# A second ScalarE activation for the high half of gelu in the last stage of a Macaron block

## The reference

```
bw1 = _binarize(w1)
h = jnp.einsum('bsd,hd->bsh', x, bw1) + b1
h = jax.nn.gelu(h, approximate=False)
bw2 = _binarize(w2)
out = jnp.einsum('bsh,dh->bsd', h, bw2) + b2
```

## Time and profile before

| what | value |
|---|---|
| median of 3 runs | 1490.82 us (1489.05 to 1491.58) |
| the profiled execution, its own time | 1486.6 us |
| its span, first to last instruction | 1484.8 us |
| PE busy | 1425.5 us (96%) |
| DVE busy | 1281.6 us (86%) |
| ACT busy | 1119.9 us (75%) |
| POOL busy | 942.8 us (64%) |
| mean granted clock of TensorE | 0.995 |

### The profile page before, as it was taken

One profiled execution on the slowest core, in us unless ns is written; L12 is line 12 of the kernel. 1 busy time (PEld: TensorE's weight loads), 2 busy tenths in 40 slices (PEclk: granted clock), 3 DMA queues, 4 the chain that ended last, 5 costly groups with the idle time before them and its releaser, 6 DMA issues. The chain is left out here.

```text
span 1484.8 us, 26133 instructions
## 1 busy us (share of the span) xinstructions
PE 1425.5 (96%) x7022; PEld 1010.8 (68%) x7022; DVE 1281.6 (86%) x2936; ACT 1119.9 (75%) x2618; POOL 942.8 (64%) x956
## 2 busy tenths in 40 slices
PE   6999999999889999999999999999999998999998
PEld 4555566555467777777777777777666666777776
DVE  7776676854689999999999999999999999788785
ACT  4554456548999999999999999999999965233333
POOL 0234322433189999999999999999999998300000
PEclk9999999999899999999999999999999999999999
DMA  8224437454766656666566656666545358464510
GB/s 278 85 83 149 148 129 194 142 164 145 240 191 187 183 162 180 185 175 179 154 175 186 183 163 173 175 171 182 127 112 120 99 134 245 139 208 150 185 56 29
DMA packets 232329, 236.33 MB, mean 159 GB/s; under 512 B 46296, under 2 KB 198040, under 8 KB 232184
## 3 DMA queue, kind: packets, MB, share of 16 engines
q1 hardware_dynamic: 231240, 233.34, 55.0%
q10 hardware_dynamic: 944, 1.31, 0.2%
HBM read 136.31 MB, written 98.56 MB: 158 GB/s over the span
## 5 line engine op out<-in xcount | busy, mean ns | idle before, releaser
L1377 DVE TENSOR_TENSOR_SCAN h<-decay,banks 128x308 f32<-128x308 f32 (+1 forms) x820 | 718.1, 882 | 0.9 <-issue 0.9
L1151 POOL TENSOR_TENSOR hc<-h,bc 128x640 f32<-128x640 f32 x410 | 592.7, 1446 | 0.0
L1200 PE MATMUL banks<-hc,w_ident 128*128 128x320 f32 (+1 forms) x1664 | 522.8, 437 | 0.1
L1269 ACT ACTIVATE tb<-dtc,a 128x320 f32<-128x320 f32 (+1 forms) x832 | 418.0, 558 | 0.0
L1200 PEld LDWEIGHTS banks<-hc,w_ident 128*128 128x128 f32 x1664 | 284.0, 191 | 66.6 <-POOL hc L1151 0.3
L1291 ACT ACTIVATE decay<-tb 128x640 f32<-128x640 f32 x410 | 296.1, 726 | 0.0
L1140 POOL TENSOR_TENSOR rc<-qs,w_mhalf 128x1 f32<-128x1 f32 x410 | 225.7, 551 | 80.2 <-DVE qs L1360 53.0
L1186 PE MATMUL banks<-ub 128*128 128x176 f32 x1640 | 272.6, 288 | 3.5 <-DMA ub<-scratch_ub 3.5
L1179 PEld LDWEIGHTS banks<-sc_ss,sc_ones 128*128 128x128 f32 x820 | 123.3, 189 | 143.2 <-ACT sc_sq L1280 141.1
L1186 PEld LDWEIGHTS banks<-ub 128*128 128x128 f32 x1640 | 216.8, 193 | 4.0 <-issue 2.5
L1367 DVE TENSOR_SCALAR banks<-h,rc 128x28 f32<-128x28 f32 (+1 forms) x820 | 176.1, 261 | 1.6 <-POOL rc L1140 1.4
(11 more groups left out here) (135 smaller groups left out, 1759.0 us busy)
## 6 DMA issues: line engine op xcount, KB each, us to landing
ub<-scratch_ub SPq DMA_DIRECT2D x410, 107.5 KB
bc<-scratch_blk SPq DMA_DIRECT2D x205, 160.0 KB, 3.5
scratch_ub<-turned SPq DMA_DIRECT2D x64, 512.0 KB, 3.6
scratch_ub<-spread SPq DMA_DIRECT2D x64, 176.0 KB, 2.4
scratch_xc<-xc SPq DMA_DIRECT2D x8, 1024.0 KB, 4.8
scratch_sg<-sg SPq DMA_DIRECT2D x8, 1024.0 KB, 5.9
piece<-scratch_u SPq DMA_DIRECT2D x32, 256.0 KB, 4.2
q_ys<-scratch_y SPq DMA_DIRECT2D x8, 1024.0 KB, 5.7
```

The costliest lines, as they stand in the source:

```text
L1151: pool.tensor_tensor(hc[:, pl % 2, :, at * S:(at + 1) * S] .rearrange("p (c b n) e -> p c b n e", c=KE, b=B)[:, :, b], state(m)[:, :, 0:S] ...
L1200: mm = pe.matmul(banks[:, y_bank(p), 0:KE * B * wide], w.ident[:], rhs, start=(n == 0), stop=(n == N - 1))
L1269: act.activation(tanh_rows(c, r), dtc[:, c % 2, k * B:(k + 1) * B, 0:blocks_of(c) * S].rearrange("p b (k e) -> p k b e", e=S), ACT.Tanh, s ...
L1377: dve.tensor_tensor_scan(state(m).rearrange("p r e -> p (r e)")[:, part], decay[:, m % DRING, part], psI[m % B][:, part], 0.0, ALU.mult, A ...
```

## The change

ScalarE gets a second kind of activation in the last stage: `high_g(i, m)`, which copies `gf` of block m as it is into the high half of g. In `gelus` it is issued for block m-1 after the gelu of block m, and for block 7 after the loop. The wait for `dn_done` goes with it. VectorE's `split_g` loses the cast and its waits and keeps the subtraction, which waits for `split_hi`, now raised by ScalarE. The orders of TensorE, GpSimd and SyncE are as they were, and so is the place of each `split_g` in VectorE's order.

```diff
@@ scalar @@
+        def high_g(i, m):
+            act.wait_ge(gelu_done, i * KH + m + 1)
+            if i >= 1 and m == 0:
+                act.wait_ge(dn_done, KD * i)
+            act.activation(g[:, 0, m, :], gf[:, m % GF, :], ACT.Copy).then_inc(split_hi, 1)
+
         def gelus(i):
             for m in range(KH):
                 act.wait_ge(up_done, i * KH + m + 1)
@@
                 act.activation(gf[:, m % GF, :], psM[:, m % 2, :], ACT.Gelu, bias=w.b1[:, m:m + 1],
                                scale=w.a1[:, m:m + 1]).then_inc(gelu_done, 1)
+                if m >= 1:
+                    high_g(i, m - 1)
+            high_g(i, KH - 1)
@@ vector @@
         def split_g(i, m0, m1):
-            if i >= 1 and m0 == 0:
-                dve.wait_ge(dn_done, KD * i)
             for m in range(m0, m1):
-                dve.wait_ge(gelu_done, i * KH + m + 1)
-                dve.tensor_copy(g[:, 0, m, :], gf[:, m % GF, :]).then_inc(split_hi, 1)
                 dve.wait_ge(split_hi, KH * i + m + 1)
                 dve.tensor_tensor(g[:, 1, m, :], gf[:, m % GF, :], g[:, 0, m, :].bitcast(F32),
                                   ALU.subtract).then_inc(split_lo, 1)
```

## The result

The changed kernel takes 1529.37 us (median of 4, 1528.3 to 1532.39) against 1491.2 for the kernel before in the same comparison: a ratio of 1.0251, with a 95% interval of 1.0219 to 1.0282. It is slower by 2.5%, and the 1531 on record lies within 2 us. As a difference of medians that is +38.2 us, where +40.5 was forecast. The profiled execution took 1528.3, its span is 1526.3, and against the profiled execution before it is +41.5 by the span.

A forecast was written before the change was run, and what follows sets the result against it. A last-stage tile was taken as bound by TensorE except for one VectorE piece after the projection. Waits of 32.1 us plus 8.4 for the clock made 40.5, on 1490.8 giving 1531 us, range 1521 to 1542.

The forecast's parts named there:

- The block at copy(5): ScalarE's copy of 5 stands behind gelu(6), which waits for the projection and `up` 6, so VectorE's subtraction of 5 waits.
- The delay of the residual: VectorE's residual, behind subtraction 5 and four skips, starts at P+5.53 instead of P+0.02 (P: projection's end, tile 1): 5.51 us.
- Last split 4.60 later: VectorE's last split in a tile ends at P+10.09 instead of P+5.49, with P the end of tile 1's projection.
- The `up` phase: A copy between gelus makes ScalarE's pitch 1.18 us, so `up` 5 and the projection come 0.28 us later.
- Tiles 0 to 5, +4.88 each in waits: Last-stage waits, 4.60 plus 0.28 us a tile, 29.3 us for six; 2.2 in tile 6 and 0.6 in tile 7.
- Signs that came out larger: Expected profile signs: VectorE waits 5 to 6 us at subtraction 5, TensorE pauses some 4.6 us before split 6.
- The clock, +8.4: TensorE's pause halves its clock in tiles 0 to 5, costing 1.4 us a tile, 8.4 in all (0 to 17).
- The removed casts are worth nothing but for 6 and 7: Casts taken off VectorE, 0.42 us each, run under TensorE's matmuls; only those of 6 and 7 delay TensorE.
- Rival 1: The block at copy(5) happens but TensorE's clock holds through the pause: 1523 us, chance 0.22.
- Rival 2: The block happens and ScalarE's copies don't overlap neighbours, pitch 1.41 us: 5.5 us more, 1537 us, chance 0.06.
- Rival 3: Not slower: subtraction 5 is done before the projection ends, and VectorE's relief at splits 6 and 7 decides: 1491 us, chance 0.03.
- Rival 4: Copies bring ScalarE table loads between gelus, 2.6 us for each m, far above the range; chance 0.01 with other large causes.

The follow-up runs named there:

- run 1: Changed kernel with the copy of block 5 issued right after the copy of 4, ahead of the gelu of 6: 1488.75 us, 0.9991 of the kernel before.
- run 5: Changed kernel with each copy issued right behind its own gelu: 1490.04 us, 0.9999 of the kernel before.
- run 6: Changed kernel with idle matmuls filling TensorE's pauses, 16 in tiles 0 to 5 and 8 in tile 6: 1523.31 us, 1.0235 of the kernel before.
- run 3: Changed kernel with 16 idle matmuls in TensorE's pause in tiles 0 to 5 only: 1525.89 us, 1.0238 of the kernel before.
- run 7: The changed kernel measured again, unaltered, in the same rounds as run 6: 1530.99 us, 1.0282 of the kernel before.
- run 4: Changed kernel with 6 idle matmuls in TensorE's pause in tiles 0 to 5: 1531.38 us, 1.028 of the kernel before.
- run 2: Changed kernel with VectorE's four skips moved ahead of its split 5: 1508.47 us, 1.0118 of the kernel before.

## Why the prediction was right

- *The block at copy(5)*: shown, by runs 1 and 5, each of which takes it away and keeps the load.
- *The delay of the residual, 5.51 us*: it starts at P+5.56 instead of P+0.02, 5.54. The subtraction of 5 starts at P+2.29 (forecast 2.27), the skips at P+2.90 (2.88). Copies last 0.62 to 0.64 us in this tile and not 0.59. That costs 0.02 us once, at the subtraction of 5, which waits for the end of its copy; the next activation starts 0.52 after a copy (0.50 on record).
- *Last split 4.60 later, at P+10.09*: measured P+10.09 (1341.79+1.29), and the normalisation hides behind it. TensorE resumes at P+9.54 (9.5).
- *The `up` phase, +0.28*: the chain has 5.37 instead of 5.08, the pitch is 1.18.
- *Tiles 0 to 5, +4.88 each in waits*: 29.79 in run 6 against 24.92, so 4.87. Tile 6 +2.22 (27.14), forecast 2.2. Tile 7, from its `up` 1 to the last addition, 17.16 against 16.55: +0.61, forecast 0.6. Waits in all: 32.1 on record, 32.0 by run 6 (33.1 less the 1.1 of the fall at its start).
- *Signs that came out larger*: VectorE's wait at the subtraction of 5 is 6.83 us where I wrote 5 to 6, and TensorE's pause 4.87 where I wrote 4.6, since `down` of 0 to 5 was done at P+4.67. Neither is a term of the sum. "The other 56 or so casts" is a slip too: 64 less two in each of seven tiles are 50, and they were priced at nothing.
- *The clock, +8.4*: it fell in all six tiles, as forecast, and cost 1.35, 1.18, 2.66, 1.83, 1.40 and 1.19 us over the 29.79 (tile 0: over 30.90, its own 26.03 with 4.87). Sum 9.6, a mean of 1.6 for my 1.4. Runs 3 and 6 take 9.4 to 9.7 away. Here is the mis-sized term: the middle of a range whose ends only one pause had shown. That the middle came this near is luck in part. The fall was expected 2.1 us into the pause and the half clock for up to 5.8 us of work behind it; in tile 1 it fell 4.4 us into the pause, and TensorE worked at half clock for 2.9 us. Read in stretches of 1 us, the half clock lasted 3.3, 2.9, 6.1, 4.4, 3.4 and 3.0 us of TensorE's work in tiles 0 to 5, and the price was in each tile half of that less 0.3 to 0.4 us.
- *The total*: the profiled executions differ by 41.5 us for a forecast of 40.5, the medians of this comparison by 38.2 and those beside run 7 by 41.9. That the 1531 lies within 2 us is finer than the totals can tell; the terms above are what bears it out.
- *The removed casts are worth nothing but for 6 and 7*: holds, run 1 is within its interval of before.
- *Rival 1 (the clock holds)* is out by run 7 and the first trace, which show every one of six pauses with a fall. *Rival 2* is out by the pitch. *Rival 3* needed the residual at the end of the projection; runs 1 and 5 build that case and give it, with 0.68 us gained at the last splits where the rival had 0.3. *Rival 4* is out: the stage still has one table load.

The Trainium skill (TensorE: Matmul & The Clock Gate, Why this matters for your kernels) warns that an idle gap between bursts of matmuls can bring back the half clock. The runs agree with it for pauses of 4.87 and 3.55 us.

What stays open is why the clock comes back late in some tiles, why the same amounts come back in both traces of the changed kernel, and why a wait of 2.21 us lowers the clock in some tiles and not in others.

## What to carry to other kernels

Before moving work to an idle engine, place it in that engine's written order and look at what stands ahead of it: here one 0.6 us copy behind an activation that waits for 7 us of unrelated matmuls cost 2.5% of a kernel, while 64 copies in the right places cost nothing. Then list what is queued behind the waiting instruction on the engine that waits, since all of it moves too, and price a pause of TensorE as the wait plus the clock behind it. Move only those pieces that the critical engine waits for: two copies of eight a tile took 4.8 us off the stage, all eight in the right places 2.0.

## What the runs showed of the hardware

- TensorE's clock behind a wait, in the last stage of these traces: a wait of 4.87 us brought it from 2.4 to 1.2 GHz in 12 of 12 cases (first trace, run 7), one of 3.55 us in 6 of 6 (run 4), one of 2.21 us in 3 of 11 (two of seven in run 2, tile 6 in run 3, none in tile 6 of the changed kernel, of run 4 and of run 7), the one of 1.90 us at the start of the stage in 3 of 10 (runs 2, 5 and 6), one of 1.12 to 1.21 us in none of 12 (runs 3 and 6). Behind the shorter waits the fall could come after TensorE had resumed: in run 6 it resumed at 1300.73 and the clock fell at about 1302.1. A fall cost 1.1 to 2.8 us and not in proportion to the wait, but to how long TensorE then worked at half clock.
- A copy from SBUF to SBUF of 128x512 with rounding took 0.62 to 0.65 us in the changed kernel, against 0.595 from PSUM in the kernel before.
- An interrupted row of matmuls costs more than its idle time shows: 0.68 us for 0.33 shown.
